# Five engines' programs for a pair of batches in attention, in a new order

## What is computed

```python
q = (x @ Wq).reshape(b, n, HEADS, DIM_HEAD)          # x is layer-normalised before
k = (context @ Wk).reshape(b, m, HEADS, DIM_HEAD)
v = (context @ Wv).reshape(b, m, HEADS, DIM_HEAD)
sim = jnp.einsum('bihd,bjhd->bhij', q, k) * SCALE
attn = jax.nn.softmax(sim, axis=-1)
out = jnp.einsum('bhij,bjhd->bihd', attn, v).reshape(b, n, HEADS * DIM_HEAD)
return out @ Wout + bout
...
x = x + _L0_xattn_ref(_layernorm(x, axis=-1), ctx_768, ...)
x = x + _L0_ffn_ref(_layernorm(x, axis=-1), ...)     # top 2 of 8 experts and a shared one
```

## Time and profile before

| | us |
|---|---|
| median of 3 executions | 1149.44 |
| the three | 1149.66, 1143.63, 1149.44 |
| span of the profiled execution | 1154.2 |
| TensorE busy in it | 1097.8 |
| VectorE, ScalarE, GpSimd busy | 766.7, 691.0, 694.4 |

### The profile page before, as it was taken

The page is one execution under the profiler, slowest core; times in us unless marked ns, Lnnn a source line. Parts: engine busy times, 40 slices in busy tenths (PEclk is TensorE's granted clock), DMA queues, the critical chain, the costliest instruction groups (busy, mean ns, idle before and its releaser), DMA issues. The chain is left out here.

```text
span 1154.2 us, 26175 instructions
## 1 busy us (share of the span) xinstructions
PE 1097.8 (95%) x7534; PEld 967.9 (84%) x7534; DVE 766.7 (66%) x2024; ACT 691.0 (60%) x1667; POOL 694.4 (60%) x629
## 2 busy tenths in 40 slices
PE   5989999999999999999999889999999999999996
PEld 4778888888888888888888779999888888888886
DVE  4778888888888888888888756675633333333332
ACT  4777777777777777777777754542233443443332
POOL 3797778768777877787787745665223333333333
PEclk9999999999999999999999998989999999999999
DMA  5223143133214322331342339222465336333861
GB/s 150 82 59 97 57 132 103 56 106 120 89 57 131 109 71 85 125 99 49 123 139 70 118 119 339 92 73 87 134 200 136 55 56 162 57 58 58 258 173 15
DMA packets 103698, 124.04 MB, mean 107 GB/s; under 512 B 19712, under 2 KB 71888, under 8 KB 103632
## 3 DMA queue, kind: packets, MB, share of 16 engines
q1 hardware_dynamic: 83376, 99.82, 26.6%
q0 software_dynamic: 11760, 15.15, 7.4%
q10 hardware_dynamic: 8496, 8.22, 2.5%
HBM read 74.40 MB, written 49.68 MB: 108 GB/s over the span
## 5 line engine op out<-in xcount | busy, mean ns | idle before, releaser
L520 POOL TENSOR_TENSOR probs<-probs,inv_sum 112x750 f32<-112x750 f32 x128 | 183.8, 1437 | 134.5 <-DVE inv_sum L974 134.4
L1726 POOL DMA_INDIRECT out<-stage,to_row x48 | 74.9, 1559 | 173.5 <-ACT stage L1778 125.2
L2006 DVE TENSOR_TENSOR hT_lo<-banks,hT_hi 128x512 fp32r<-128x512 f32 x63 | 43.6, 691 | 184.5 <-ACT hT_hi L1770 178.6
L690 ACT ACTIVATE probs<-banks,neg_max 112x375 f32<-112x375 f32 x256 | 145.9, 573 | 18.3 <-DVE neg_max L961 15.4
L961 DVE TENSOR_REDUCE neg_max<-banks 112x2 f32<-112x750 f32 x128 | 119.8, 936 | 47.7 <-PE banks L1320 46.0
L487 POOL TENSOR_TENSOR v_both<-v_raw,v_both 125x512 fp32r<-125x512 f32 x96 | 123.2, 1284 | 7.5
L1346 PE MATMUL banks<-ident,probs 112*125 112x112 f32 x768 | 106.9, 275 | 12.7 <-DVE pT L967 12.7
L1334 PE MATMUL banks<-pT,v_both 125*128 125x224 f32 x768 | 114.0, 284 | 5.1 <-DVE oT_lo L992 5.0
L1334 PEld LDWEIGHTS banks<-pT,v_both 125*128 125x128 f32 x768 | 99.2, 192 | 23.2 <-issue 21.4
L967 DVE TENSOR_TENSOR pT<-banks,pT 125x672 fp32r<-125x672 f32 x128 | 108.6, 849 | 14.4 <-ACT pT L681 13.1
L1346 PEld LDWEIGHTS banks<-ident,probs 112*125 112x125 f32 x768 | 97.0, 189 | 24.1 <-issue 20.0
(11 more groups left out here) (292 smaller groups left out, 3206.0 us busy)
## 6 DMA issues: line engine op xcount, KB each, us to landing
w_split_scratch<-stage SPq DMA_DIRECT2D x16, 1536.0 KB, 8.2
ring<-w_split_scratch SPq DMA_DIRECT2D x16, 1536.0 KB
stage<-in_L_ffn_W SPq DMA_DIRECT2D x48, 256.0 KB, 2.9
ctx_in<-in_ctx SPq DMA_DIRECT2D x32, 281.2 KB
xg<-x_sorted_scratch ACTq DMA_DIRECT2D x59, 136.0 KB
x_in<-in_x SPq DMA_DIRECT2D x16, 224.0 KB, 2.5
x_res<-in_x SPq DMA_DIRECT2D x32, 112.0 KB, 2.1
x_scratch<-x SPq DMA_DIRECT2D x32, 112.0 KB, 1.9
```

The lines of the kernel that those rows point to most:

```text
L520: pool.tensor_tensor(probs[:, two, :], probs[:, two, :], inv_sum[:, 2 * s:2 * s + 2].rearrange("p (e o) -> p e o", o=1).to_broadcast([N, 2 ...
L690: act.activation(probs[:, h % 4, :], S_BANKS[0:N, e, 0:M], ACT.Exp, bias=neg_max[:, h:h + 1], accum_out=row_sum[:, h:h + 1]).then_inc(exp_ ...
```

## The change

The table `UNITS` and the order of the calls in `body(p)` on TensorE, ScalarE, VectorE, GpSimd and SP are new. The last pair's text and the prologue stay. No instruction is added or taken away, no buffer changes; one wait moves with the order (that for `c10` stands at `k10`, which is now the first `k` unit of the next pair's first batch). The diff, with the bodies of ScalarE, VectorE and GpSimd left out:

```diff
@@ -36,8 +36,8 @@
 
 UNIT_BANKS = 3
 PROLOGUE = ["c00", "c10", "k00", "k10", "k20", "k30", "v00", "xt0", "xt1", "v10", "q0", "c01", "c11"]
-UNITS = ["v20", "k01", "k21", "q1", "k11", "c00", "v01", "v11", "w1", "xt0", "c10", "v21", "k31", "xt1", "k20",
-         "k00", "k10", "k30", "v00", "q0", "w0", "v10", "c01", "c11"]
+UNITS = ["v20", "k01", "q1", "k21", "k11", "c00", "k31", "c10", "v01", "v11", "w1", "xt0", "k10", "k20", "xt1",
+         "k00", "v21", "q0", "c01", "v00", "k30", "c11", "v10", "w0"]
...
@@ -409,25 +409,24 @@
 
             def body(p, two_more=True):
                 first = isinstance(p, int) and p == 0
+                if not first:
+                    sp.wait_ge(half_lo, 3 * p)
+                    store_half(p - 1)
+                    store(2 * p - 1, 1, done_count(p, False, "w1"))
                 if two_more:
                     sp.wait_ge(xn_ready, p + 2)
                     sp.dma_start(x_in[:], x_rows(2 * p + 4, 2)).then_inc(x_loaded, 16)
+                sp.wait_ge(stage_free, 16 * p + 16)
+                load_half(p)
                 if not first:
-                    store(2 * p - 1, 1, done_count(p, False, "w1"))
                     sp.dma_start(x_res[1][:], batch_of(2 * p + 1)).then_inc(res_loaded[1], 16)
                 if two_more:
+                    sp.wait_ge(unit_made, unit_count(p, False, "c11"))
+                    load_ctx(2 * p + 5, 1)
                     sp.wait_ge(unit_made, unit_count(p, False, "c10"))
                     load_ctx(2 * p + 4, 0)
                 store(2 * p, 0, done_count(p, False, "w0"))
                 sp.dma_start(x_res[0][:], batch_of(2 * p + 2)).then_inc(res_loaded[0], 16)
-                if two_more:
-                    sp.wait_ge(unit_made, unit_count(p, False, "c11"))
-                    load_ctx(2 * p + 5, 1)
-                if not first:
-                    sp.wait_ge(half_lo, 3 * p)
-                    store_half(p - 1)
-                sp.wait_ge(stage_free, 16 * p + 16)
-                load_half(p)
 
             body(0)
             with sp.Fori(1, PAIRS - 2) as p:
...
@@ -1281,7 +1280,7 @@
                     pe.wait_ge(xn_ready, p + 2)
                 if name[0:2] == "c0":
                     pe.wait_ge(ctx_loaded[batch_in(name)], 32 * (p + 2))
-                if name == "k20":
+                if name == "k10" and not last:
                     pe.wait_ge(unit_done, done_count(p, last, "c10"))
                 if name == ("k31" if last else "k01"):
@@ -1349,56 +1348,56 @@
 
             def body(p):
                 first = isinstance(p, int) and p == 0
+                scores(p, False, 0)
                 run(p, False, "v20")
-                scores(p, False, 0)
                 run(p, False, "k01")
                 if not first:
                     turn_probs(p - 1, 7)
                     sums(p - 1, 6)
+                scores(p, False, 1)
+                run(p, False, "q1")
                 run(p, False, "k21")
-                run(p, False, "q1")
-                scores(p, False, 1)
                 run(p, False, "k11")
+                scores(p, False, 2)
+                run(p, False, "c00")
+                turn_probs(p, 0)
                 if not first:
                     sums(p - 1, 7)
-                run(p, False, "c00")
+                run(p, False, "k31")
+                run(p, False, "c10")
                 run(p, False, "v01")
-                scores(p, False, 2)
-                turn_probs(p, 0)
+                scores(p, False, 3)
+                turn_probs(p, 1)
                 run(p, False, "v11")
-                turn_probs(p, 1)
-                scores(p, False, 3)
                 sums(p, 0)
                 run(p, False, "w1")
...
```

More of the change, by code:

```diff
@@ L546, in body @@
                 first = isinstance(p, int) and p == 0
-                normalise(p, 0)
                 run(p, False, "v20")
                 rstd_of(p + 2)
[L550 to L556, removed]
+                normalise(p, 0)
                 if not first:
                     split_piece(p - 1, 0)
+                normalise(p, 1)
+                if not first:
                     add_bout(0, p + 1)
-                normalise(p, 5)
+                normalise(p, 2)
+                run(p, False, "v01")
+                normalise(p, 3)
                 if not first:
                     split_piece(p - 1, 1)
+                normalise(p, 4)
+                run(p, False, "v11")
+                if not first:
+                    split_piece(p - 1, 2)
+                run(p, False, "v21")
+                normalise(p, 5)
                 normalise(p, 6)
@@ L696, in body @@
                     high_of_probs(p - 1, 6)
+                exponential(p, 0, 0)
+                exponential(p, 0, 1)
                 run(p, False, "v20")
                 run(p, False, "k01")
[L699 to L702, removed]
                 if not first:
                     copy_cross(p - 1, 6)
-                run(p, False, "k21")
+                    high_of_probs(p - 1, 7)
+                    hi_of_piece(p - 1, 0)
+                exponential(p, 1, 0)
                 run(p, False, "q1")
@@ L708, in body @@
                     high_of_sums(p - 1, 6)
+                exponential(p, 1, 1)
+                run(p, False, "k21")
                 run(p, False, "k11")
-                exponential(p, 1, 0)
                 if not first:
-                    copy_cross(p - 1, 7)
-                exponential(p, 1, 1)
+                    hi_of_piece(p - 1, 1)
                 run(p, False, "c00")
-                run(p, False, "v01")
-                if not first:
-                    high_of_sums(p - 1, 7)
                 high_of_probs(p, 0)
@@ L767, in body @@
-                run(p, False, "c11")
                 high_of_sums(p, 5)
@@ L1021, in body @@
                 first = isinstance(p, int) and p == 0
+                maximum(p, 0)
                 if not first:
                     low_of_probs(p - 1, 6)
-                maximum(p, 0)
                 statistics(p + 2)
-                run(p, False, "k01")
-                if not first:
-                    low_of_probs(p - 1, 7)
                 reciprocal(p, 0)
@@ L1365, in body @@
+                run(p, False, "c10")
                 run(p, False, "v01")
-                scores(p, False, 2)
-                turn_probs(p, 0)
+                scores(p, False, 3)
+                turn_probs(p, 1)
                 run(p, False, "v11")
-                turn_probs(p, 1)
-                scores(p, False, 3)
                 sums(p, 0)
                 run(p, False, "w1")
+                scores(p, False, 4)
+                turn_probs(p, 2)
+                sums(p, 1)
                 run(p, False, "xt0")
-                turn_probs(p, 2)
@@ L1375, in body @@
-                run(p, False, "c10")
-                scores(p, False, 4)
-                sums(p, 1)
-                run(p, False, "v21")
-                run(p, False, "k31")
-                turn_probs(p, 3)
-                scores(p, False, 5)
-                run(p, False, "xt1")
-                run(p, False, "k20")
-                sums(p, 2)
-                run(p, False, "k00")
+                run(p, False, "k10")
+                run(p, False, "k20")
+                scores(p, False, 5)
@@ L1386, in body @@
+                turn_probs(p, 3)
+                sums(p, 2)
+                run(p, False, "xt1")
+                run(p, False, "k00")
+                run(p, False, "v21")
+                scores(p, False, 6)
                 turn_probs(p, 4)
-                scores(p, False, 6)
-                run(p, False, "k10")
                 sums(p, 3)
-                run(p, False, "k30")
-                run(p, False, "v00")
-                run(p, False, "q0")
-                scores(p, False, 7)
@@ L1394, in body @@
-                sums(p, 4)
-                turn_probs(p, 5)
-                run(p, False, "w0")
-                run(p, False, "v10")
-                sums(p, 5)
-                run(p, False, "c01")
-                run(p, False, "c11")
-                turn_probs(p, 6)
+                run(p, False, "q0")
+                run(p, False, "c01")
+                run(p, False, "v00")
+                scores(p, False, 7)
+                turn_probs(p, 5)
+                sums(p, 4)
+                run(p, False, "k30")
@@ L1403, in _ @@
+                run(p, False, "c11")
+                run(p, False, "v10")
+                turn_probs(p, 6)
+                sums(p, 5)
+                run(p, False, "w0")
             rounds(pe, body)
```

109 lines of the change are left out of this document (56 added, 53 removed).

## The result

The changed kernel takes 1143.14 us (median of 15 runs, 1141.31 to 1145.95) against 1148.22 for the kernel before beside it (15 runs, 1142.85 to 1150.19): ratio 0.996, 95% interval 0.9949 to 0.9971. That is 5.1 us, inside the 0.5% that I called the same, but the forecast was 1152 with a range that began at 1145: it moved the other way and fell out of the range.

The account below looks back on a forecast made before the run. TensorE, 98% busy, was taken to set the time, so only its waits could be won. 11.4 us lost once less 9.1 gained over thirteen pairs gave +2.3 on 1149.4: 1151.7, say 1152 us; range 1145 to 1160.

Parts of the forecast that it names:

- The pair's gain: Thirteen equal pairs: 1.2 us won less 0.3 for borders and 0.2 for new waits, 0.7 a pair, 9.1 us.
- The true price of the two waits: TensorE's waits at `turn_probs(p, 1)` and `sums(p-1, 7)`, shown as 0.63 and 0.25 us, forecast to cost 1.2 a pair.
- the seven more borders: TensorE's changes between transposes, scores and other products, 22 before and 29 after, taken to cost 0.3 us a pair.
- new waits, 0.2 a pair: Waits the new order might bring in each pair where room is small: 0.2 us, range 0 to 0.6.
- The places with 0.05 to 0.2 us of room: Six or seven places in a pair, such as step 2's scores behind `q_lo`, where not all were expected to hold.
- The loss once: Pair 1: context loads issued behind the first half's load, so `c00` waits until 86 us; 11.4 us lost.
- the half clock behind it: Pair 1: after TensorE's long idle the granted clock falls from 2.4 to 1.2 GHz, costing 1.7 us.
- The last pair, put at 0 together with the prologue and pair 0: Prologue, pair 0 and the last pair's order were taken to stay about as they are: 0 us.
- The waits did not come back: Rival: late low parts on VectorE return the pairs' waits elsewhere; at full return +11.4, 1161 us; chance 0.20.
- `c00` did not wait in every pair: Rival: `c00` waits for its context in every pair, its load following the half's; +11.4, 1161 us; chance 0.10.
- The first load was late: Rival judged: the first context load is not late or its wait is hidden; 1143 us; chance 0.06.
- The level: Forecast started from the three runs' median, 1149.44 us, not the profiled span of 1154.2, 4.8 us higher.

Follow-up runs that it names:

- the run with the piece alone: Changed kernel with ScalarE's high part of the half's first piece moved behind step 1's exponentials, SP's order as in the change: ratio 0.9975.
- the one with the filler moved: Kernel before with projection `w1` on TensorE moved between `v11` and step 1's transposes, instead of behind `sums(0)`: ratio 1.003, +3.8 us.
- the run that takes it away: Changed kernel with SP's old order in pair 14 alone, the half's store and load last: 1148.68 us, ratio 1.0003 to the kernel before.
- the run with SP's order in the kernel before: Kernel before with SP's new order from pair 1 on, pair 0 keeping its old one: ratio 1.1538, +178.5 us.
- the one with the half first: Kernel before with SP's new order in pair 0 only, first half's load ahead of both context loads: ratio 1.0101, +11.3 us.

## Why the prediction was wrong

- **The pair's gain** was 0.94 us where I had 0.7, thirteen times 12.3 instead of 9.1. The true price of the two waits was right: `v11` takes 1.24 us without a wait (524.12 to 525.36 in the new trace; forecast 1.25) and 2.03 with it, so 0.79; a `k` unit between scores and sums takes 0.96 without a wait (535.35 to 536.31 in the old trace) and 1.37 with it, so 0.41; 1.20 together, as forecast. 1.20 - 0.94 leaves 0.26 for the seven more borders, where I took 0.3; this is a remainder, which also holds any wait too short to be recorded, and no run measured it alone. The term that failed is "new waits, 0.2 a pair": there is one of 0.15 us in thirteen pairs. The places with 0.05 to 0.2 us of room held, as far as waits are recorded. Worth 2.6 us.
- **The loss once** was 12.2 where I had 11.4. Its cause, its place on SP, the landing (87.06 against 86) and the half clock behind it (0.50 in the mean from 82 to 87, 0.53 from 87 to 91) were right: from `c00` to pair 2 it takes 31.6 us where the working had 30.1 and 1.7. I missed that ScalarE stands behind the same half. It costs nothing extra in the changed kernel, as the run with the piece alone shows, but it takes half of the repair. And 12.2 is measured against a trace in which the clock stayed up behind step 7's wait. In the three other traces of the old order with that wait it falls, and the one with the filler moved pays 2.8 us for it, so against another execution of the kernel before the loss may be some 3 us smaller.
- **The last pair, put at 0 together with the prologue and pair 0**, is the step that turned the sign. The last pair gains 3.8 us by the first two traces (2.2 to 3.9 by all) and 4.5 in the run that takes it away, because SP loads the last half at 621.23 instead of 634.17. I had that row, and the wait of 1.82 us, and used the one for a rival and the other for the clock. I read the last pair by its code, which does not change, and not by what reaches it from the pair before. Pair 0 lost 0.8 us (pair 1 starts at 64.47 instead of 63.65), which lies inside the 12.2.
- **Sum.** -12.3 + 12.2 - 3.8 = -3.9 us against +2.3 on record; the medians say -5.1, with an interval of -5.9 to -3.3. Two steps make up the whole miss from +2.3 to -3.9: 3.2 from the pairs (2.6 of it the new waits), 3.8 from the last pair, 0.8 back. The 1.2 us between -3.9 and -5.1 lie inside the interval; that clock would make a difference of this sign, but no run shows it for the medians.
- **The rivals.** The waits did not come back. `c00` did not wait in every pair; the run with SP's order in the kernel before shows that it would have with the pieces in their old order, some 14 us later in a pair. The working took 27 us into a pair for the third piece, and the new trace shows that. The first load was late.
- **The level.** The span of the profiled execution had an experts' part 10 us longer than on the chips where the kernel takes 1148 us. That did no harm, since I moved from the median and not from the span, but the 12.2 us between the two traces would have misled anyone who took them for the change.

## What to carry to other kernels

When an order is changed on a queue in a loop, read its ends as well as its body: the first pass meets a signal that is late once, and the passes behind the loop inherit its loads earlier or later, though their own code stays. A wait seen behind a late signal has others hidden beside it; follow the signal and move its source, here the shared split, rather than each waiter. And where an edit on one engine depends on others, as SP's order on the pieces' here, it alone can cost over thirty times what all bring (178.5 us against 5.1).

## What was not expected of the hardware

- The experts' part, the same instructions in every kernel, lasts 457.3 to 458.1 us on some chips and 467.2 to 471.6 on others, and the whole kernel before 1146.6 to 1148.2 or 1158.0 to 1159.0. Attention's equal pairs in the new order differ by less than 0.03 us (39.10 to 39.13). What in the chips makes the difference stays open.
- The second context load's issue itself takes SP long when it follows the half and the first context: 2.59 and 2.20 us above, where the first part of a lone one takes 0.28. In the equal pairs too (2.02 and 1.63 us at 547.26 and 549.48); whatever is queued behind it on SP pays this.
- Behind the same wait the clock falls or stays. After 2.45 us at step 7's transposes in pair 1 it is 1.00 from 69.2 to 73 us in the kernel before, 0.50 from 71 to 73 in the one with the half first, whose TensorE program is the same, and 0.57 from 69.2 to 76.2 in the one with the filler moved.
- The clock moves the last stretch by steps that no edit explains: from the last context's transposes to the experts' start the traces show 11.7, 13.3 or 14.9 us in kernels whose code there is the same, and 14.9 and 13.2 in two traces of the changed kernel; the granted clock from 660 to 690 us is 0.94 in the kernel before and 0.89 in the changed one.
